# Diagonal score tiles decayed by VectorE straight out of PSUM and squared in place, and ScalarE rounding the experts' hidden tiles

## The reference, cut to what matters

```
# attention: 16 query heads of 64, 8 key/value heads, B = 2
s      = einsum('bthd,bshd->bhts', q, k) * scale
logits = 2 * log(abs(s) + 1e-30) + log_G[:, :, :, None] - log_G[:, :, None, :]
logits = where(mask, logits, -inf)                      # causal
a      = where(mask, exp(logits - max(logits)), 0)      # = s^2 * decay(t, s) / its row's maximum
y      = einsum('bhts,bshd->bthd', a, v) / (sum(a) + 1e-6)
...
# experts: each token goes to 2 of 8, each expert takes at most 1280 tokens
y_e = gelu(x_e @ W1[e] + b1[e]) @ W2[e] + b2[e]         # 256 -> 1024 -> 256
y   = y.at[idx].add(y_e * w)
```

## Time and profile before

| | |
|---|---|
| median of 3 runs | 2451.53 us (2450.71 to 2457.05) |
| the profiled execution, own time | 2438.49 us |
| its span | 2436.7 us |
| attention, us of the span | 355 to 1530 |
| experts, us of the span | 1857 to 2406 |
| busy in the span: PE, DVE, ACT, POOL | 2164.7, 2015.0, 1298.7, 1361.9 us |
| granted clock of PE, mean | 0.953 |

### The profile page before, as it was taken

One profiled execution on the slowest core, in us unless ns is written; L12 is line 12 of the kernel. 1 busy time (PEld: TensorE's weight loads), 2 busy tenths in 40 slices (PEclk: granted clock), 3 DMA queues, 4 the chain that ended last, 5 costly groups with the idle time before them and its releaser, 6 DMA issues. The chain is left out here.

```text
span 2436.7 us, 45915 instructions
## 1 busy us (share of the span) xinstructions
PE 2164.7 (89%) x12401; PEld 1331.9 (55%) x12401; DVE 2015.0 (83%) x2913; ACT 1298.7 (53%) x2108; POOL 1361.9 (56%) x1042
## 2 busy tenths in 40 slices
PE   7888879999999999999999999699837989899894
PEld 5666643333333333333333333599726989899894
DVE  6888858899899888989889898677688878788783
ACT  4555557667677666667667666244303433344431
POOL 4777735565566555656555555266535555555453
PEclk9999989999999999999999999899957999999997
DMA  4444460222211222211222201344332333333334
GB/s 164 125 123 121 125 186 16 79 74 73 79 42 45 78 73 74 78 49 38 78 74 73 78 29 58 103 132 131 119 111 49 79 79 71 62 72 79 75 77 97
DMA packets 192739, 205.35 MB, mean 84 GB/s; under 512 B 44392, under 2 KB 169520, under 8 KB 185584
## 3 DMA queue, kind: packets, MB, share of 16 engines
q1 hardware_dynamic: 159952, 156.00, 21.2%
q0 software_dynamic: 15840, 22.29, 5.8%
q10 hardware_dynamic: 16768, 25.17, 3.3%
HBM read 132.64 MB, written 74.97 MB: 85 GB/s over the span
## 5 line engine op out<-in xcount | busy, mean ns | idle before, releaser
L906 DVE TENSOR_TENSOR att_sb_acc<-att_sb_acc,att_sb_a 128x1024 f32<-128x1024 f32 (+3 forms) x576 | 794.3, 1405 | 37.4 <-ACT att_sb_a L867 11.9
L867 ACT ACTIVATE att_sb_a<-att_ps_s,att_sb_fg,att_sb_f 128x1024 f32<-128x1024 f32 x384 | 461.4, 1202 | 318.6 <-PE att_ps_s L994 314.2
L809 POOL TENSOR_TENSOR att_sb_a<-att_sb_a,att_sb_dec 128x1024 f32<-128x1024 f32 (+3 forms) x256 | 486.6, 1909 | 221.6 <-ACT att_sb_a L872 221.5
L796 POOL TENSOR_SCALAR_AFFINE_SELECT att_sb_dec<-att_sb_dec 128x128 f32<-128x128 f32 x256 | 190.2, 745 | 284.9 <-ACT att_sb_dec L847 283.6
L994 PE MATMUL att_ps_s<-first_sb_q,first_sb_k 64*128 64x512 f32 (+3 forms) x1292 | 289.2, 563 | 20.2 <-DVE keep_sb_row_max L934 13.6
L994 PE MATMUL att_ps_s<-att_sb_q,att_sb_k 64*128 64x512 f32 (+3 forms) x1280 | 279.9, 554 | 0.5
L1602 POOL DMA_INDIRECT total<-ffn_sb_ys,ffn_sb_add_now x80 | 128.3, 1604 | 220.0 <-DVE ffn_sb_ys L1779 207.8
L994 PEld LDWEIGHTS att_ps_s<-first_sb_q,first_sb_k 64*128 64x128 f32 x1292 | 112.0, 189 | 205.0 <-issue 108.5
L872 ACT ACTIVATE att_sb_a<-att_ps_s,att_sb_guard 128x1024 f32<-128x1024 f32 (+3 forms) x256 | 198.2, 787 | 45.1 <-PE att_ps_s L994 45.1
L1658 ACT ACTIVATE ffn_sb_h<-ffn_ps_p,ffn_sb_b_cols 128x256 f32<-128x256 f32 x320 | 142.8, 470 | 135.3 <-DVE ffn_sb_h_lo L1760 110.5
L994 PEld LDWEIGHTS att_ps_s<-att_sb_q,att_sb_k 64*128 64x128 f32 x1280 | 109.0, 186 | 179.2 <-issue 104.3
(11 more groups left out here) (249 smaller groups left out, 4078.2 us busy)
## 6 DMA issues: line engine op xcount, KB each, us to landing
ffn_sb_raw<-L_ffn_W ACTq DMA_DIRECT2D x36, 512.0 KB, 4.0
att_sb_hb<-half_log SPq DMA_DIRECT2D x17, 1024.0 KB, 12.2
close_sb_nT<-num_rows SPq DMA_DIRECT2D x34, 512.0 KB, 4.0
q_rows<-proj_sb_rT SPq DMA_DIRECT2D x64, 256.0 KB, 2.3
num_rows<-att_sb_num SPq DMA_DIRECT2D x64, 256.0 KB, 2.1
first_sb_q<-q_rows SPq DMA_DIRECT2D x9, 1024.0 KB, 5.7
first_sb_k<-k_rows SPq DMA_DIRECT2D x18, 512.0 KB, 8.5
v_cent<-proj_sb_vt SPq DMA_DIRECT2D x32, 256.0 KB, 2.4
```

The source lines that it names most:

```text
L796: nc.gpsimd.affine_select(out=tile, in_=tile, compare_op=ALU.is_ge, fill=0.0, base=0, pattern=[[1, P]], channel_multiplier=-1).then_inc(de ...
L809: nc.gpsimd.tensor_tensor(x, x, dec[:, own_slot(i), j, None, 0:TB - j * P].to_broadcast([P, 2, TB - j * P]), ALU.mult).then_inc(mul_done, 1)
L867: nc.scalar.activation(a[:, g % A, :, :], s_ps[slot(n)][:, :, :], ACT.Square, scale=f[:, p, i - 1, s:s + 1], bias=fg[:, p, i - 1, s:s + 1] ...
L906: nc.vector.tensor_tensor(x[:, :, c:TB], x[:, :, c:TB], a[:, g % A, :, c:TB], ALU.max).then_inc(max_done, 1)
```

## The change

In attention a diagonal tile is now multiplied before it is squared. ACT computes `dec` with half the exponent (so `nfull`, the doubled logarithms, is gone). DVE reads the scores in PSUM, adds the guard and multiplies by `dec` into `a` in one instruction (`own_scores`, placed at n + 0.6 in DVE's order); ACT then squares `a` in place. POOL only masks. PE's wait for a diagonal tile's slot goes to `own_done`, the new instruction. The first off tile of a block is no longer copied; the maximum of the first and the second opens the block. LAG goes from 6.5 to 4.5, which sets values and maxima of diagonal tiles two steps earlier.

In the experts ACT writes `h_hi` (one Gelu later than the Gelu it belongs to), DVE keeps `h_lo`; `h` has 8 tiles in place of 4, so a Gelu waits for the `h_lo` of a whole group before. ACT's gate rows stand behind the Gelus, DVE's gate rows ahead of its inputs, and PE's `down` waits for the bias addition (`sum_done`) and no longer for the product behind it (`y_done`).

```
-LAG = 6.5
+LAG = 4.5
...
                         if kind == "diag":
-                            g = sq_of[n]
-                            pool.wait_ge(dec_done, ready(q * ND + decay_base[i] + j))
-                            pool.wait_ge(sq_done, ready(q * NS + g))
-                            x = a[:, g % A, :, j * P:TB]
-                            nc.gpsimd.tensor_tensor(x, x, dec[:, own_slot(i), j, None, 0:TB - j * P].to_broadcast([P, 2, TB - j * P]),
-                                                    ALU.mult).then_inc(mul_done, 1)
...
                 nc.scalar.activation(dec[:, own_slot(i), j, 0:w], hb[p][:, i * TB + j * P:(i + 1) * TB], ACT.Exp,
-                                     scale=2.0, bias=nfull[:, p, i * ST + j:i * ST + j + 1]).then_inc(exp_done, 1)
+                                     bias=nh[:, p, i * ST + j:i * ST + j + 1]).then_inc(exp_done, 1)
...
                             else:
-                                nc.scalar.activation(a[:, g % A, :, s * P:TB], s_ps[slot(n)][:, :, s * P:TB], ACT.Square,
-                                                     bias=guard[:, :]).then_inc(sq_done, 1)
+                                act.wait_ge(own_done, ready(q * ND + own_of[n]))
+                                nc.scalar.activation(a[:, g % A, :, s * P:TB], a[:, g % A, :, s * P:TB], ACT.Square).then_inc(sq_done, 1)
...
+            def own_scores(q, p, n):
+
+                kind, i, j = steps[n]
+                d, w = own_of[n], TB - j * P
+                dve.wait_ge(s_done, ready(q * N + n))
+                dve.wait_ge(dec_done, ready(q * ND + decay_base[i] + j))
+                g = sq_of[n]
+                free_at = ready(use_of[squares[(g - A) % NS]] + (q if g >= A else q - 1) * NS)
+                dve.wait_ge(av_done, free_at)
+                dve.wait_ge(max_done, free_at)
+                nc.vector.scalar_tensor_tensor(a[:, g % A, :, j * P:TB], s_ps[slot(n)][:, :, j * P:TB], GUARD,
+                                               dec[:, own_slot(i), j, None, 0:w].to_broadcast([P, 2, w]),
+                                               ALU.add, ALU.mult).then_inc(own_done, 1)
...
+            todo += [(n + 0.6, 5, n) for n in diags]
...
                     pe.wait_ge(row_done, ready((q - back) * NB + m_of[k]))
+                elif steps[k][0] == "diag":
+                    pe.wait_ge(own_done, ready((q - back) * ND + own_of[k]))
...
-        h = m.sbuf("h", [P, RING, W])
+        h = m.sbuf("h", [P, KI, W])
...
+                    def upper(k):
+                        u = (e * NG + g) * KI + k
+                        if k == 0:
+                            act.wait_ge(y_mm, ready((e * NG + g - 1) * GT - 1))
+                        act.wait_ge(up_done, ready(u))
+                        nc.scalar.activation(h_hi[:, G % 2, k, :], h[:, k, :], ACT.Copy).then_inc(h_hi_done, 1)
...
-                        nc.vector.tensor_copy(h_hi[:, G % 2, k, :], piece).then_inc(h_hi_done, 1)
...
-                        pe.wait_ge(y_done, free(e * XT + t, 2))
+                        pe.wait_ge(sum_done, free(e * XT + t, 2))
```

More of the change, by code:

```diff
@@ L753, in attend @@
         LOADS = 16 * 5
-        s_done, sq_done, mul_done, av_done, max_done, row_done, num_done, scaled, part_done = (
-            m.sem(s) for s in ("s", "sq", "mul", "av", "max", "row", "num", "scaled", "part"))
+        s_done, sq_done, own_done, av_done, max_done, row_done, num_done, scaled, part_done = (
+            m.sem(s) for s in ("s", "sq", "own", "av", "max", "row", "num", "scaled", "part"))
         block = ctx.enter_context(nc.Block())
@@ L892, in maximum @@
                 g, u = sq_of[n], use_of[n]
[L893 to L896 removed]
                 x = acc[:, acc_slot(i, p), :, :]
                 c = s * P if kind == "diag" else 0
[L899 removed]
+                if kind == "off" and s == 0:
+                    return
+                dve.wait_ge(sq_done, ready(q * NS + g))
+                if kind == "diag" and s == 0 and i == 0:
                     nc.vector.tensor_copy(x, a[:, g % A, :, :]).then_inc(max_done, 1)
+                elif kind == "off" and s == 1:
+                    first = sq_of[at["off", i, 0]]
+                    nc.vector.tensor_tensor(x, a[:, first % A, :, :], a[:, g % A, :, :], ALU.max).then_inc(max_done, 2)
                 else:
@@ L951, in _ @@
                             before_own(q, p, x)
+                        elif what == 5:
+                            own_scores(q, p, x)
                         else:
@@ L1647, in _ @@
                     e = it * 2 + p
+                    def upper(k):
[4 more added lines that the diff above has]
+                        nc.scalar.activation(h_hi[:, G % 2, k, :], h[:, k, :], ACT.Copy).then_inc(h_hi_done, 1)
+                    for k in range(KI):
+                        u = (e * NG + g) * KI + k
+                        act.wait_ge(up_mm, ready(u))
+                        act.wait_ge(h_lo_done, free(u, KI))
+                        apart(act, keep)
+                        nc.scalar.activation(h[:, k, :], p1[(G * KI + k) % RING][:, :], ACT.Gelu,
+                                             bias=b1_cols[:, bass.ds(e * KI + k, 1)]).then_inc(up_done, 1)
+                        if k:
+                            upper(k - 1)
+                    upper(KI - 1)
                     for t in range(g * GT, (g + 1) * GT):
@@ L1652, in _ @@
                                              scale=weight[:, 1, bass.ds(e * XT + t, 1)]).then_inc(gate_done, 1)
-                    for k in range(KI):
-                        u = (e * NG + g) * KI + k
-                        act.wait_ge(up_mm, ready(u))
-                        act.wait_ge(h_lo_done, free(u, RING))
-                        apart(act, keep)
-                        nc.scalar.activation(h[:, (G * KI + k) % RING, :], p1[(G * KI + k) % RING][:, :], ACT.Gelu,
-                                             bias=b1_cols[:, bass.ds(e * KI + k, 1)]).then_inc(up_done, 1)
                     for c in ((0, 1), (), (2, 3), ())[g] if g < 4 else ():
@@ L1667, in _ @@
         def _(dve):
-            for s in (sum_done, hot_done, token_done, read_done, add_done, w_lo_done, x_hi_done, x_lo_done, h_hi_done, h_lo_done, y_done):
+            for s in (sum_done, hot_done, token_done, read_done, add_done, w_lo_done, x_hi_done, x_lo_done, h_lo_done, y_done):
                 dve.sem_inc(s, CREDIT)
@@ L1772, in outputs @@
                                                        gate[:, slot, :], ALU.mult, ALU.add)
+                def outputs(p, G, g):
+                    e, tiles = it * 2 + p, tiles_of(p, G, g)
+                    if g == 0:
+                        dve.wait_ge(b2_in[p], it * 16 + 16)
                     for n, slot, i in tiles:
```

46 lines of the change are left out of this document (16 added, 30 removed).

## The result

| | before | after |
|---|---|---|
| median | 2452.15 us | 2469.18 us (2468.8 to 2470.62, 4 runs) |
| ratio | | 1.0067, 95% interval [1.005, 1.0084] |
| span of the profiled execution | 2436.7 us | 2467.1 us |
| attention, us of the span | 355 to 1530 | 355 to 1616 |
| experts, us of the span | 1857 to 2406 | 1944 to 2434 |

What follows compares the result with a forecast made beforehand. Attention was taken as bound by PE, with 33 us of waits to win, and the experts as PE's work plus 79 us of stalls. Experts -64 and attention +34 gave -30 from 2451.5, so 2422 us, range 2375 to 2462.

Steps and rivals of the forecast that it cites:

- the term of the new waits: Attention: PE waits for DVE 3.2 and 0.2 us at a pair's end, 0.8 at block 2's begin; 67 us in all.
- 33 us of old ones: Attention: PE's present waits for DVE, 33 us together, were to go since DVE is no longer held.
- The tail's working: End of a pair: DVE's queue 6.3 us plus 0.25 for the semaphore, against PE's 2.8 and 0.5; PE waits 3.2.
- The reads of PSUM: Attention: DVE's new reads take 1.22 us for 1024 columns, 0.42 for the smallest tiles, 13 us a pair.
- DVE freed from POOL: Attention: without POOL's multiplies a pair's maxima fall from 50 to 38 us, DVE's sum from 65 to about 64.
- The experts: Experts stage: 79 us of stalls less 15 that stay, so a gain of 64 us.
- 8 tiles and a whole up of slack: Experts: the argument against half the stall staying; h's 8 tiles and one up (5.7 us) cover a held h_lo.
- the gate rows' new places: Experts: the moved gate rows go with the change and have no price of their own.
- Rival 1: Attention: the slot loop decides, PE's scores late throughout; 103 us longer at 8.5 us a pair, kernel 2490; chance 0.12.
- Rival 2: Attention: DVE freed from POOL keeps up, stage 14 us shorter, kernel 2373 us; chance 0.20.
- Rival 3: Experts: the hold only moves to h_lo, ACT and PE wait half as much; gain 32, time 2453; chance 0.10.
- Rival 4: Attention: not bound by PE, DVE's 64 us set a pair; 144 us less there, kernel 2244; chance 0.02.

Runs made afterwards that it cites:

- e4: The changed kernel with PE computing the scores of each pair's last diagonal tile 15 times over instead of once; 2434.93 us, ratio 0.9947.
- e3: The changed kernel with DVE's two remaining reads of PSUM at each pair's end ahead of the maxima (order only); 2395.06 us, ratio 0.9777.
- e7: The kernel before with the whole change in the experts alone, but h a ring of 4 tiles as before; 2389.3 us, ratio 0.9735.
- e8: The kernel before with only h given 8 tiles in place of 4; 2451.69 us, ratio 0.9994.
- e12: The kernel before with only ACT's two gate rows of a group moved behind its eight Gelus; 2407.93 us, ratio 0.983.
- e5: e3 with DVE also closing the off part of blocks 2 and 3 ahead of the scaling; 2380.81 us, ratio 0.9705.
- e9: e5 with DVE closing block 1's off part behind the third read of PSUM at a pair's end; 2377.88 us, ratio 0.9699.
- e10: e9 with DVE's loop over pairs in 4 turns of 4 pairs in place of 8 of 2; 2372.14 us, ratio 0.9689.
- e6: The changed kernel with LAG 6.5 as before; 2456.58 us, ratio 1.0013.

## Why the prediction was wrong

**The step that failed** is the term of the new waits, "Together 4.2 us a pair, 67 us in 16", against 33 us of old ones. It was mis-sized in two ways. The waits themselves are 84 us: 3.49 or 3.84 at the tail where 3.2 and 0.2 stood, 1.24 at the off part where 0.8 stood, and 0.56 to 1.13 more at the start of seven pairs, 5.7 in all; net 51 us in place of 34. The larger part of the error is a cost that had no term at all: behind the wait at the tail PE works at the lower clock, 1.6 to 2.5 us a pair and 34 in 16 (e4), and its busy time in attention grew by 38 us. New waits and clock together are 85 to 89 us; attention grew by 86. e3 takes the clock's part and two thirds of the tail's wait away with an edit of DVE's order alone, e4 the clock's part.

**The tail's working** was right in both of its sums. DVE's queue is 6.4 us (6.3 forecast). PE's side was forecast as 3.3 us from the end of the first diagonal scores to the last values, and it is that: these scores are 4 matmuls (in the timeline up to 971.5) that end at 971.75, and PE's last values end at 975.05.

```profile
970.62 1.13 PE L1005 MATMUL att_ps_s<-att_sb_q,att_sb_k 64*128 64x512 f32 x4
```

What the wait was short of lies at the two ends: DVE starts 0.3 us behind those scores in one pair and 0.64 in the next (0.25 forecast), and PE starts 0.12 us behind the end of the third read, for which nothing stood. So 0.64 + 6.38 + 0.12 - 3.30 is the 3.84 of the pair shown. Why every second pair starts 0.35 us later was not followed.

**The reads of PSUM** take 1.22 us for 1024 columns and 0.41 for 256, as taken from the earlier trace rows. The rule of the Trainium skill ("VectorE: DVE Perf Modes", the TRN2 errata) that a PSUM source costs 62 cycles more does not show: the maximum out of SBUF is 1.22 at the median too. The Square from SBUF is 736 ns on the mean against 787 from PSUM, where no change was forecast.

**DVE freed from POOL**: the longest maximum is 1.23 us (3.40 before). DVE lost 59 us, 3.7 a pair; 1 a pair was forecast. The waits that this was to save came back elsewhere, as the order at the tail is what counts.

**The experts** took 59 us less, as forecast (64), for reasons half of which are wrong. "8 tiles and a whole up of slack" was the argument, and e7 and e8 show that the tiles do nothing. That "the gate rows' new places" are among what was to "have no price of their own" was the sentence that failed: e12 makes ACT's gate rows 42 of the 66 us. That the sum was near is in this part luck. The row was at hand: the earlier trace rows shows a gate row waiting 5.96 us for DVE with the Gelus behind it. That DVE's own load counts (the copy's 20 us) and that h_lo is held instead, up to 6.18 us where 3 to 6 stood, came as said.

**Rivals.** Rival 1 was right in its bound (slower from 6.1 us a pair; with the clock's part, which it did not have, it was (84 + 34) / 16 = 7.4) and wrong in its place: ACT's standing in line behind DVE at every diagonal tile still costs 219 us of ACT's time in e3, and attention is only 13 us over before there. Rival 2 (DVE keeps up, 2373) is what the same instructions give once the tail is in another order: e5, e9 and e10, 2372 to 2381. Rival 3 fell by the experts' 490 us. Rival 4 fell as well: PEld is busy 34% of the changed attention, and yet 39 us less of PE's waits and 34 us less of its busy time shortened the stage by 68 us in e3, so PE bounds it. The rule of the Trainium skill ("Perfetto Trace Analysis", Identifying the Most-Contended Engine) to judge its headroom by LDWEIGHTS busy does not carry over to this stage.

## What to carry to other kernels

When a wait of some microseconds is put on PE, price the wait and the work behind it, and read the granted clock there: here a wait of 3.7 us on the mean cost 5.8. When an engine takes over the release of a buffer, write out its queue at the place where the waiting engine runs out of other work, and move what nobody waits for behind the release; the mean load of the two engines did not show it here. And in a stage with a held instruction, look for what stands in order in front of the critical work and waits for the held engine: moving two rows gave 42 us, moving the load on top of it 20, and a deeper buffer by itself nothing.

## What the hardware showed that was not expected

More work made the kernel faster: 56 matmuls in a gap kept the granted clock at 1.00 and gave 29 us (e4). Behind tail waits of 3.49 and 3.84 us the clock fell in all 16 pairs, behind those of 3.33 us in 11 of 16 (e6). Of the four waits of 1.8 to 2.1 us in e9 two were followed by it (1.83 and 1.92 us) and two were not (2.03 and 2.12), so these traces give no length of a wait that decides.

DVE stops without a releaser for 2.1 to 4.0 us at most borders between turns of its loop over pairs, 145 us apart, and 289 apart with turns twice as long (e9, e10). The Trainium skill ("Runtime: NRT & Kernel Launch", Instruction fetch mechanics) says that a taken branch breaks the prefetch of instructions; the places agree with it, and no run here shows the fetch itself. The kernel before has the same stops, up to twice at a border:

```profile
DVE att_sb_acc L900 <- issue: 13.6, 6, 2.3
DVE att_sb_acc L906 <- issue: 6.7, 3, 2.3
```

Behind them stands, in its timeline, PE's wait for the reduction of the earlier trace rows (1.1 to 2.4 us at seven borders), which the forecast had put down to the holds. In e9, where POOL multiplies nothing, PE still waits 1.5 to 2.1 us at five of the seven borders, so not all of the 33 us of old waits were owed to POOL.
